# Audio tower layer: part of the feed-forward's integer products on GpSimd, from int32 operands

## The reference

```python
def act_qdq(x):
    qmax = 2.0 ** (ACT_BITS - 1) - 1.0
    scale = jnp.maximum(jnp.max(jnp.abs(x)) / qmax, 1e-12)
    return jnp.clip(jnp.round(x / scale), -qmax - 1.0, qmax) * scale
...
x = act_qdq(x)
up = act_qdq(x @ lpbq_dequant(w_up).T)
gate = act_qdq(x @ lpbq_dequant(w_gate).T)
sig = fixed_qdq_u16(jax.nn.sigmoid(gate))
gate = act_qdq(gate * sig)
o = act_qdq(gate * up)
return o @ lpbq_dequant(w_down).T
```

## Time and profile before

| | |
|---|---|
| median of 3 runs | 801.94 us (795.84 to 803.84) |
| the profiled execution | 800.07 us |
| its span in the trace | 798.1 us |
| gate stage, from VectorE's first product to the end of its last maximum | 588.80 to 664.52 us |
| output stage, likewise | 667.75 to 721.51 us |

### The profile page before, as it was taken

The page is one execution under the profiler, slowest core; times in us unless marked ns, Lnnn a source line. Parts: engine busy times, 40 slices in busy tenths (PEclk is TensorE's granted clock), DMA queues, the critical chain, the costliest instruction groups (busy, mean ns, idle before and its releaser), DMA issues. The chain is left out here.

```text
span 798.1 us, 14680 instructions
## 1 busy us (share of the span) xinstructions
PE 620.4 (78%) x5169; PEld 466.2 (58%) x5169; DVE 603.7 (76%) x967; ACT 452.2 (57%) x647; POOL 134.3 (17%) x211
## 2 busy tenths in 40 slices
PE   4577989899998989898997975989999800006998
PEld 3446777777777777777775743434444300004997
DVE  7425888788888888898888767687479998994442
ACT  1424544665456654664466353436389966967772
POOL 4211232113311332123311000000024320000000
PEclk9789999999999999999999775999999955555999
DMA  7323213231333123331323102000134144400533
GB/s 201 114 29 48 42 21 60 49 60 27 46 46 59 36 37 51 54 53 20 61 41 54 54 14 83 9 1 1 68 140 182 58 175 155 130 0 1 149 116 100
DMA packets 39204, 52.82 MB, mean 66 GB/s; under 512 B 5724, under 2 KB 31772, under 8 KB 39164
## 3 DMA queue, kind: packets, MB, share of 16 engines
q1 hardware_dynamic: 38012, 51.49, 26.0%
q10 hardware_dynamic: 1152, 0.79, 0.4%
HBM read 22.74 MB, written 16.81 MB: 50 GB/s over the span
## 5 line engine op out<-in xcount | busy, mean ns | idle before, releaser
L816 DVE TENSOR_REDUCE mx<-ps 126x2 f32<-126x504 f32 (+1 forms) x192 | 125.6, 676 | 52.4 <-PE ps L668 50.9
L892 ACT ACTIVATE pt<-sbr 126x504 f32<-126x504 f32 x192 | 114.9, 617 | 26.0 <-DVE sbr L807 24.8
L807 DVE TENSOR_TENSOR sbr<-ps,biasT 126x504 f32<-126x504 f32 x192 | 120.0, 675 | 7.7 <-PE ps L686 7.2
L665 PE MATMUL ps<-biasN,antib 126*126 126x504 bf16 x192 | 74.9, 390 | 26.8 <-DMA k_st<-kl 26.8
L668 PE MATMUL ps<-k_st,q_st 65*126 65x252 f16 (+1 forms) x512 | 75.2, 249 | 0.0
L1159 PE MATMUL ps<-x2t,wgT 128*128 128x504 f16 x288 | 67.2, 394 | 8.1 <-ACT gat L1450 4.7
L1436 PE MATMUL ps<-wdT,raws 128*126 128x256 f16 x480 | 67.6, 283 | 4.5 <-DVE raws L1377 4.5
L668 PEld LDWEIGHTS ps<-k_st,q_st 65*126 65x126 f16 x512 | 60.6, 140 | 17.9 <-issue 3.4
L1135 PE MATMUL ps<-identf,sc 128*128 128x128 f32 x5 | 2.2, 434 | 86.7 <-DVE sc L1367 56.5
L686 PE MATMUL ps<-q_st,k_st 66*126 66x252 f16 (+1 forms) x512 | 68.4, 254 | 0.6 <-DMA q_st<-mneg 0.6
L977 POOL TENSOR_TENSOR h<-h,bc 126x512 f32<-126x512 f32 x16 | 20.4, 1277 | 269.4 <-ACT h L915 269.4
(11 more groups left out here) (189 smaller groups left out, 1471.3 us busy)
## 6 DMA issues: line engine op xcount, KB each, us to landing
up_raw<-raws SPq DMA_DIRECT2D x11, 756.0 KB, 3.2
x2t<-up_raw SPq DMA_DIRECT2D x6, 756.0 KB, 6.6
q_st<-qh SPq DMA_DIRECT2D x32, 128.0 KB, 4.0
k_st<-kh SPq DMA_DIRECT2D x32, 128.0 KB, 4.0
res<-hall SPq DMA_DIRECT2D x16, 252.0 KB
x2t<-res SPq DMA_DIRECT2D x16, 252.0 KB
out<-x2t SPq DMA_DIRECT2D x16, 252.0 KB
raws<-up_raw SPq DMA_DIRECT2D x5, 756.0 KB, 4.1
```

Source lines behind the costliest of these rows:

```text
L665: nc.tensor.matmul(dst, antib[0:TT], biasN[0:TT, heads[0]:heads[-1] + 1, N - w:N], start=True, stop=True)
L807: nc.vector.tensor_tensor(sbr[0:TT, n % 4].rearrange("p (h w) -> p h w", w=w), ps[0:TT, score_bank[name, n], 0:2 * N].rearrange("p (h w) - ...
L816: nc.vector.tensor_reduce(mx[0:TT, 0 if w == TT else 1, heads[0]:heads[-1] + 1], ps[0:TT, score_bank[name, n], 0:2 * N].rearrange("p (h w) ...
L892: nc.scalar.activation(pt[0:TT, n // 3 % 2, n % 3], sbr[0:TT, n % 4], ACT.Exp).then_inc(S["exp_r"], 1)
```

## The change

Seven gate products (tiles 1, 3, 5, 7, 9, 11, 13, `P_POOL`) and five output products (steps 1, 4, 7, 10, 13, `O_POOL`) move from VectorE to GpSimd. GpSimd multiplies two int32 tiles into an int32 tile; the result takes the place of the float tile in `gat`, and VectorE's maxima and ScalarE's next conversion read it as int32. For these tiles ScalarE writes the integers as int32 into wide slots: for the gate two (`wide`: the storage of the gate's weights and the first columns of the quantised input), for the output stage one slot for each operand (`wide[0]` and `wide2`, the storage of the up weights). GpSimd also makes the gate integers of tiles 4, 8 and 12 (`GQ_POOL`) and the up integers of steps 2, 5, 8, 11 and 14 (`UQ_POOL`), which were ScalarE's. The clamp at 65535 moves from VectorE's product into GpSimd's conversion. VectorE takes the maximum of a product of GpSimd's one tile later than that of its own. Products and integers of the two engines are counted by semaphores of their own (`pp_r`, `pgq_r`, `po_r`, `puq_r`), and SyncE's reload additionally waits for the last two gate products of GpSimd, because the first reloaded tile lands in the storage of the second wide slot.

```diff
+        wide = [wgT[:].rearrange("p a k n -> p (a k n)").bitcast(I32)[:, 0:UW], xf[:, 0:UW].bitcast(I32)]
+        wide2 = wuT[:].rearrange("p a k n -> p (a k n)").bitcast(I32)[:, 0:UW]
+
+
+        P_POOL, GQ_POOL = list(range(1, TL - 1, 2)), list((4, 8, 12))
+        O_POOL, UQ_POOL = list(range(1, TL - 1, 3)), list(range(2, TL, 3))
+
+        def done_of(eng, t, by_pool, other, pool_name):
+
+            if t < 0:
+                return
+            before = sum(i <= t for i in by_pool)
+            wait(eng, *((pool_name, before) if t in by_pool else (other, t + 1 - before)))
...
+        def gq_of(t):
+            return wide[P_POOL.index(t) % 2] if t in P_POOL else gq[t % 3][:]
+
+        def gq_free(eng, t):
+
+            if t in P_POOL:
+                i = P_POOL.index(t)
+                p_done(eng, P_POOL[i - 2] if i >= 2 else -1)
+            else:
+                p_done(eng, max([i for i in range(t) if i not in P_POOL and i % 3 == t % 3], default=-1))
+
+        def p_of(t):
+            return gat[:, t].bitcast(I32) if t in P_POOL else gat[:, t]
+
+        def o_of(n):
+            return gat[:, TURN[n]].bitcast(I32) if n in O_POOL else gat[:, TURN[n]]
...
         def uq_slot(n):
-            return gq[(n + 1) % 3][:]
+            return wide[0] if n in O_POOL else gq[(n + 1) % 3][:]
+
+        def g2_slot(n):
+            return wide2 if n in O_POOL else g2[n % 3]
 
         def uq_free(eng, n):
 
-            if n < 3:
-                wait(eng, "p_r", TL - 2 + n)
+            if n in O_POOL:
+                i = O_POOL.index(n)
+                if i == 0:
+                    p_done(eng, P_POOL[-1])
+                    p_done(eng, P_POOL[-2])
+                else:
+                    o_done(eng, O_POOL[i - 1])
+            elif n < 3:
+                p_done(eng, max(t for t in range(TL) if t not in P_POOL and t % 3 == (n + 1) % 3))
             else:
-                wait(eng, "o_r", n - 2)
+                o_done(eng, n - 3)
...
+                def largest_p(t):
+                    p_done(dve, t)
+                    nc.vector.tensor_reduce(amax[:, 2, t:t + 1], p_of(t), X, ALU.max,
+                                            apply_absolute_value=True).then_inc(S["ap_r"], 1)
+
                 for t in range(TL):
-                    wait(dve, "sq_r", t + 1)
-                    wait(dve, "gq_r", t + 1)
-                    nc.vector.scalar_tensor_tensor(gat[:, t], sq[t % 2][:], 65535.0, gq[t % 3][:], ALU.min,
-                                                   ALU.mult).then_inc(S["p_r"], 1)
+                    if t not in P_POOL:
+                        wait(dve, "sq_r", t + 1)
+                        gq_done(dve, t)
+                        nc.vector.scalar_tensor_tensor(gat[:, t], sq[t % 2][:], 65535.0, gq_of(t), ALU.min,
+                                                       ALU.mult).then_inc(S["p_r"], 1)
                     if t + 3 < TL:
                         largest_up(t + 3)
-                    wait(dve, "p_r", t + 1)
-                    nc.vector.tensor_reduce(amax[:, 2, t:t + 1], gat[:, t], X, ALU.max,
-                                            apply_absolute_value=True).then_inc(S["ap_r"], 1)
+                    if t - 1 in P_POOL:
+                        largest_p(t - 1)
+                    if t not in P_POOL:
+                        largest_p(t)
...
-                    wait(dve, "o_r", n + 1)
-                    nc.vector.tensor_reduce(amax[:, 3, n:n + 1], gat[:, TURN[n]], X, ALU.max,
+                    o_done(dve, n)
+                    nc.vector.tensor_reduce(amax[:, 3, n:n + 1], o_of(n), X, ALU.max,
                                             apply_absolute_value=True).then_inc(S["ao_r"], 1)
 
                 for n in range(TL):
-                    wait(dve, "uq_r", n + 1)
-                    wait(dve, "g2_r", n + 1)
-                    nc.vector.tensor_tensor(gat[:, TURN[n]], g2[n % 3], uq_slot(n), ALU.mult).then_inc(S["o_r"], 1)
-                    if n >= 1:
+                    if n not in O_POOL:
+                        uq_done(dve, n)
+                        wait(dve, "g2_r", n + 1)
+                        nc.vector.tensor_tensor(gat[:, TURN[n]], g2_slot(n), uq_slot(n), ALU.mult
+                                                ).then_inc(S["o_r"], 1)
+                    if n >= 1 and n - 1 not in O_POOL:
                         largest_o(n - 1)
+                    if n >= 2 and n - 2 in O_POOL:
+                        largest_o(n - 2)
...
                 for t in range(TL):
-                    wait(act, "p_r", t - 2)
-                    nc.scalar.activation(gq[t % 3][:], gat[:, t], ACT.Copy, scale=col["inv_g"]
-                                         ).then_inc(S["gq_r"], 1)
-                    wait(act, "gq_r", t + 1)
+                    if t not in GQ_POOL:
+                        gq_free(act, t)
+                        nc.scalar.activation(gq_of(t), gat[:, t], ACT.Copy, scale=col["inv_g"]
+                                             ).then_inc(S["gq_r"], 1)
+                    gq_done(act, t)
                     wait(act, "sq_r", t - 1)
-                    nc.scalar.activation(sig[t % 2][:], gq[t % 3][:], ACT.Sigmoid, scale=col["size_g"]
+                    nc.scalar.activation(sig[t % 2][:], gq_of(t), ACT.Sigmoid, scale=col["size_g"]
                                          ).then_inc(S["sig_r"], 1)
                     if t + 3 < TL:
                         take(t + 3)
@@ -1501,10 +1567,13 @@
                 up_integers(0)
                 wait(act, "sc_r", scalars_at["inv_p"])
                 for n in range(TL):
-                    if n > 0:
+                    if n > 0 and n not in UQ_POOL:
                         up_integers(n)
-                    wait(act, "o_r", n - 2)
-                    nc.scalar.activation(g2[n % 3], gat[:, TURN[n]], ACT.Copy, scale=col["inv_p"]
+                    if n in O_POOL:
+                        uq_free(act, n)
+                    else:
+                        o_done(act, n - 3)
+                    nc.scalar.activation(g2_slot(n), p_of(TURN[n]), ACT.Copy, scale=col["inv_p"]
                                          ).then_inc(S["g2_r"], 1)
...
             def _(pool):
 
+                wait(pool, "sc_r", scalars_at["size_g"])
                 for t in range(TL):
                     wait(pool, "sig_r", t + 1)
-                    wait(pool, "p_r", t - 1)
-                    nc.gpsimd.tensor_scalar(sq[t % 2][:], sig[t % 2][:], 65536.0, 0.0, ALU.mult, ALU.add
+                    p_done(pool, t - 2)
+                    nc.gpsimd.tensor_scalar(sq[t % 2][:], sig[t % 2][:], 65536.0, 65535.0, ALU.mult, ALU.min
                                             ).then_inc(S["sq_r"], 1)
+                    if t + 1 in GQ_POOL:
+                        gq_free(pool, t + 1)
+                        nc.gpsimd.tensor_scalar(gq_of(t + 1), gat[:, t + 1], col["inv_g"], 0.0, ALU.mult, ALU.add
+                                                ).then_inc(S["pgq_r"], 1)
+                    if t in P_POOL:
+                        wait(pool, "sq_r", t + 1)
+                        gq_done(pool, t)
+                        nc.gpsimd.tensor_tensor(p_of(t), sq[t % 2][:], gq_of(t), ALU.mult).then_inc(S["pp_r"], 1)
+                wait(pool, "sc_r", scalars_at["inv_u"])
+                for n in range(TL):
+                    if n in UQ_POOL:
+                        raw_there(pool, n)
+                        uq_free(pool, n)
+                        nc.gpsimd.tensor_scalar(uq_slot(n), raw_of(n), col["inv_u"], 0.0, ALU.mult, ALU.add
+                                                ).then_inc(S["puq_r"], 1)
+                    if n in O_POOL:
+                        uq_done(pool, n)
+                        wait(pool, "g2_r", n + 1)
+                        nc.gpsimd.tensor_tensor(o_of(n), g2_slot(n), uq_slot(n), ALU.mult).then_inc(S["po_r"], 1)
 
             @block.sync
             def _(sp):
@@ -1539,16 +1628,19 @@
                     wait(sp, "raw_r", t + 1)
                     sp.dma_start(up_raw.ap()[t // 2, t % 2], raw[t % RING]).then_inc(S[f"raw_out{t % RING}"], 16)
                 wait(sp, "u_ps", TL)
+                p_done(sp, P_POOL[-2])
+                p_done(sp, P_POOL[-1])
                 for t in range(SPILLED):
                     wait(sp, f"raw_out{t % RING}", 16 * (t // RING + 1))
                     if t >= 5:
-                        wait(sp, "uq_r", t - 4 if t < 10 else TURN.index(0) + 1)
+                        uq_done(sp, t - 5 if t < 10 else TURN.index(0))
```

More of the change, by code:

```diff
@@ L104, in audio_tower @@
             wo_ps h2_r spilled bns2_r mv2_r ve2_r rstd2_r nb2_r nm2_r nm_r xn2_r x2T_ps x2_r ax_r
-            xi_r xqh_r xq_r ag_r ared par sc_r ap_r ao_r oq_r oh_r ol_r
+            pp_r pgq_r po_r puq_r xi_r xqh_r xq_r ag_r ared par sc_r ap_r ao_r oq_r oh_r ol_r
             g_ps g_r u_ps raw_r au_r gq_r sig_r sq_r p_r g2_r uq_r o_r""".split()
```

(18 more changed lines are left out.)

## The result

The changed kernel takes 845.9 us (median of 4 runs, 845.1 to 849.4) against 799.5 us for the kernel before (median of 4 runs, one more than in the table above): ratio 1.0593, 95% interval 1.0552 to 1.0634. It is 46 us slower. The forecast was 803.8 us with a range of 792 to 818, most likely within 1%; the measured time lies 28 us above that range.

What follows compares the result with a forecast made beforehand. Both stages were taken as bound by VectorE's instruction count, with its products and GpSimd's instructions excluding each other. From 800.07 us, 2.4 gained in the gate stage and 6.1 lost in the output stage gave 803.8, range 792 to 818.

Steps and rivals of the forecast that it cites:

- The step that failed: Gate stage: GpSimd's conversions clamp at no extra pass, so 19 one-input instructions at 1.45 us make 27.6 us.
- the bounds: GpSimd's int32 product: at least the one-input instruction's 1.45 us, at most twice 3.47, 6.9 us.
- Rival 3: GpSimd's integer product is dear, 4.6 us in the middle of that case, giving 816 us; chance 0.20.
- the power row: Profile row on GpSimd: a power on 2 columns costs 0.702 us, a sum 0.195; cited for a dear integer product.
- The frame: Gate stage: GpSimd's instructions and VectorE's remaining products cannot overlap, together 63.4 us; the stage gains 2.4 us.
- The product's price: A GpSimd int32 product over 1512 columns takes 3.47 us, drawn out from float rows of 2, 256 and 512 columns.
- First come, first served: Output stage: a waiting GpSimd instruction gets in between two back-to-back VectorE products; VectorE waits 3.5 us each time.
- The 0.05 us: Gate stage: after a VectorE product ends, the waiting GpSimd is in 0.05 us before VectorE's next instruction starts.
- The three waits: Output stage: GpSimd's products 7, 10 and 13 each hold VectorE up 3.5 us, 10.5 us in all.
- rival 1: Output stage: VectorE keeps its turn between back-to-back products, the stage takes 49.4 us, the kernel 793.3 us; chance 0.18.
- the idle 4.5 us: Output stage: VectorE idles 4.5 us after its first maximum, until GpSimd has made product 1 and tile 2's up integers.
- the reload: SyncE's reload of five spilled tiles waits for GpSimd's product 13, at about 651, hidden by some 20 us.

Runs made afterwards that it cites:

- run 1: Changed kernel with GpSimd's conversion back to multiply and add zero, so no clamp for the seven tiles of GpSimd's product: 793.2 us, ratio 0.9908 to the kernel before.
- run 7: Changed kernel without the clamp in the conversion, and with float32 for int32 in wide slots, GpSimd's products and those tiles' conversions: 796.6 us in one run.
- run 6: Kernel before with only the output part of the change, conversion with add zero, plus a second pair of wide slots: 806.4 us in one run, beside 798.5.
- run 3: Kernel before with GpSimd's sixteen conversions taking six forms in turn (multiply with add, minimum or maximum, or alone): 814.2 us in one run.
- run 2: Kernel before with GpSimd's conversion as multiply and minimum, nothing moved to GpSimd: 823.3 us in one run.

## Why the prediction was wrong, step by step

- *The step that failed* is the half sentence "the conversions now clamp at 65535 at no extra pass". It set 19 x 1.45 us where 16 x 5.29 + 3 x 1.53 were due, 61.7 us more on the list that bounds the stage; 56.2 of them came out (the stage was to gain 2.4 and lost 53.8), most of the rest because two products slipped under the end of a conversion, 1.4 us each, and the second conversion no longer waited its 1.2. The kernel before had no minimum on GpSimd and at this size only multiply-add, and the bounds were given to the new product, not to the edited old instruction. Rival 3 had the right mechanism, an operation's kind that multiplies GpSimd's price, with the power row as its sign, and put it on the product.
- *The frame held for the changed kernel*: GpSimd's list plus VectorE's products bound the gate stage, 32.6 of 33.0 us over four tiles. With the clamp gone, the stage gains 3.6 us where 2.4 had been reckoned, but that it comes so close is luck: of the 11.5 us for VectorE's products 1.2 show as waits of GpSimd, while GpSimd waits 12.8 us for ScalarE where 1.2 were reckoned (run 1). The forecast had ScalarE lying beside; there it waits for GpSimd's gate integers, and GpSimd for its sigmoids.
- *The product's price held*: 3.47 us taken, 3.38 to 3.42 measured, and float costs the same (run 7). The figure of the Trainium skill (GPSIMD Engine Reference, section 3.1) gives by columns an estimate of 3.32 us, and the trace's 3.38 to 3.42 agrees with it. That float products and sums cost the same is so in the trace (1.28 us for L977's product, 1.26 for L980's sum), but the earlier trace rows, cited for it, shows no product.
- *First come, first served held*, but it was applied to the wrong moment, and this is the second step that failed. The 0.05 us given for it proves little, since VectorE's next instruction there was a maximum, and no row shows one held up. Run 6 shows that a waiting GpSimd product does go in between and costs the 3.2 us; in the change itself it became ready just after VectorE's second product had begun. The three waits, 10.5 us of the sum, hung on some tenths of a microsecond that the list of durations did not resolve. The stage gained 4.9 us where 6.1 were to be lost; the stage came out as under rival 1 (49.4 us, 48.9 measured), but not for its reason.
- *The small ones held*: the idle 4.5 us (4.36), the reload (issued at 696.83, right behind GpSimd's product 13, and nothing in the output stage waits for it), the maxima on int32 data at 1.64 us a piece.

## What to carry to other kernels

Price an edited instruction like a new one: on GpSimd a change of one operation at the same size made 1.45 us into 5.29, so a form that no row shows needs both bounds even where it looks like a constant exchanged. Where two engines exclude each other, add up both lists over one period; that sum carried to within 2% in the changed kernel, where GpSimd had no gap. Where it has gaps, look for the third engine that it waits for. And where an instruction of the one becomes ready at about the moment at which the other's next one starts, look at both outcomes and at what decides them; more buffering can bring on the bad one.

## What was not expected of the hardware

- On GpSimd a one-input instruction over 128 x 1512 columns takes 1.45 us as multiply and add, 4.03 us as multiply alone, and 5.30 us with a minimum in either place or a maximum in the second (run 3). Why is open; no run here looks inside.
- The 5.29 us form lets a two-input VectorE instruction in 1.4 us before it ends (run 2 and the changed kernel), and multiply alone at least 1.0 us before (run 3: started at 649.67, the conversion's end at 650.66). A GpSimd product does so only 0.13 us before (run 6: VectorE in at 689.60, the product's end at 689.73), and so does the multiply-add form (618.28 + 2.43 - 1.72 = 618.99 against 619.13). The Trainium skill (SBUF — State Buffer, "Who interferes with whom") has the shared pair held for the whole instruction; for the 5.29 us form the measurement says 3.9 of 5.3 us.
- Between two back-to-back VectorE products a waiting GpSimd product is served first and the second VectorE product waits 3.2 us (run 6). What a clamp costs on ScalarE, or on VectorE as an instruction of its own, was not tried.
